# Mixture-of-experts up-projections as three float32r products of split operands, and the ternary weights in three in-place passes

## The reference

```
x = layernorm(x).reshape(1024, 512)
probs = softmax(x @ gate_w.T)              # 8 experts
topk_w, topk_idx = top_k(probs, 2)         # weights then normed to sum 1
h = silu(x @ w1[e]) * (x @ w3[e])          # w1, w3: (8, 512, 1024) float32
y = h @ w2[e]                              # w2: (8, 1024, 512) float32
out = sum over the two experts of topk_w * y
```

```
s = 1 / clip(mean(abs(w)), 1e-5)
w_q = clip(round(w * s), -1, 1) / s        # w_gate, w_up: (2048, 512); w_down: (512, 2048)
```

## Time and profile before

| | us |
|---|---|
| median of 3 runs | 1607.39 |
| runs | 1606.76, 1607.39, 1616.51 |
| span of the profiled execution | 1614.2 |
| mean granted clock of TensorE over it | 0.912 |

### The profile page before, as it was taken

How to read it: one execution, slowest core, us unless ns; L and a number is a source line. 1 busy time by engine, 2 the same in 40 slices (tenths; PEclk the granted TensorE clock), 3 DMA queues, 4 the chain that set the end, 5 groups by cost and what they waited for, 6 DMA issues and landing times.

```text
span 1614.2 us, 23219 instructions
## 1 busy us (share of the span) xinstructions
PE 1381.5 (86%) x8228; PEld 705.0 (44%) x8228; DVE 1002.9 (62%) x1708; ACT 820.5 (51%) x1176; POOL 425.7 (26%) x317
## 2 busy tenths in 40 slices
PE   8993888898847999999999999776777787779786
PEld 4441555555524444444444444333444343444333
DVE  6997999999974011110111101698989999885973
ACT  5775888888830111011110111218888898882574
POOL 1114100000004657999950000301111111110340
PEclk9996999999978999999999999887777777779998
DMA  9995354544247999999997996379887878883001
GB/s 290 295 292 142 89 133 113 134 113 117 63 157 277 385 350 370 370 396 399 404 365 295 317 354 261 110 157 201 167 174 152 171 155 179 156 149 79 1 1 52
DMA packets 452746, 338.40 MB, mean 210 GB/s; under 512 B 366360, under 2 KB 368408, under 8 KB 452032
## 3 DMA queue, kind: packets, MB, share of 16 engines
q1 hardware_dynamic: 438384, 291.31, 63.0%
q0 software_dynamic: 9920, 37.75, 6.3%
q10 hardware_dynamic: 4368, 8.39, 1.4%
HBM read 205.86 MB, written 38.01 MB: 151 GB/s over the span
## 4 chain that ended last, share of the span: by engine, by line
PE 52%; DVE 28%; issue 10%; ACT 5%; POOL 2%; DMA 2%; POOLq 0%; DVEq 0%; ACTq 0%
PE scores L1062 17%; DVE arena L1915 11%; PE bank L1080 9%; PE scores L1133 4%; PE bank L945 4%; DVE arena L1702 2%; PE scores L928 2%; PE scores L929 2%; PE bank L1180 2%; DVE arena L1688 2%; ACT arena L1377 2%; PE scores L1242 1%; PE bank L1278 1%; PE scores L1072 1%; PE scores L1162 1%
## 5 line engine op out<-in xcount | busy, mean ns | idle before, releaser
L1915 DVE TENSOR_SCALAR_CACHE_REDUCE arena<-scores,arena 128x1024 f32<-128x1024 f32 x256 | 314.6, 1279 | 32.0 <-PE scores L1133 30.6
L1062 PE MATMUL scores<-arena 128*128 128x512 f32 x736 | 319.7, 592 | 0.0
L1476 ACT ACTIVATE arena<-arena 128x2048 int16<-128x2048 f32 x128 | 273.6, 2149 | 78.5 <-POOL arena L828 41.9
L1838 DVE TENSOR_TENSOR arena<-scores,arena 128x512 f32<-128x512 f32 x46 | 31.8, 692 | 442.6 <-PE scores L1062 442.6
L1133 PE MATMUL scores<-arena 96*128 96x512 bf16 x512 | 193.2, 486 | 86.3 <-DVE arena L1915 81.6
L1062 PEld LDWEIGHTS scores<-arena 128*128 128x128 f32 x736 | 139.8, 190 | 175.8 <-issue 175.5
L1080 PE MATMUL bank<-arena 128*128 128x512 f32 x368 | 164.7, 601 | 3.4 <-issue 3.3
L1425 ACT ACTIVATE arena<-scores 128x512 f32<-128x512 f32 x46 | 27.5, 597 | 209.7 <-PE scores L1062 209.7
L1688 DVE TENSOR_REDUCE arena<-scores 128x1 f32<-128x640 f32 (+3 forms) x128 | 127.7, 1019 | 4.8 <-PE scores L906 4.4
L1377 ACT ACTIVATE arena<-scores 128x512 f32<-128x512 f32 (+3 forms) x256 | 116.6, 506 | 26.0 <-PE scores L929 25.0
L1702 DVE TENSOR_TENSOR arena<-arena 128x1024 f16<-128x1024 f32 (+2 forms) x128 | 126.2, 1026 | 3.5 <-ACT arena L1384 3.4
(11 more groups left out here) (285 smaller groups left out, 2160.0 us busy)
## 6 DMA issues: line engine op xcount, KB each, us to landing
arena<-in_L_ffn_w SPq DMA_DIRECT2D x69, 2048.0 KB, 12.6
arena<-arena SPq DMA_DIRECT2D x32, 256.0 KB, 2.9
kst_d<-arena POOLq DMA_DIRECT2D x16, 384.0 KB, 5.5
tern_d<-arena POOLq DMA_DIRECT2D x12, 512.0 KB, 7.0
arena<-kst_d SPq DMA_DIRECT2D x16, 384.0 KB, 4.0
xs_d<-arena SPq DMA_DIRECT2D x23, 256.0 KB, 2.9
arena<-xs_d SPq DMA_DIRECT2D x22, 256.0 KB, 13.0
ys_d<-arena ACTq DMA_DIRECT2D x22, 256.0 KB, 7.0
```

Of the source, the lines that this page charges most:

```text
L1062: ins = pe.matmul(scores[:, m * 1024 + half * 512:m * 1024 + half * 512 + 512], xsT[a][:, c], wa[:, m, c, half * 512:half * 512 + 512], st ...
L1476: act.activation(dst, src, ACT.Exp, bias=ebias[n % SBUFS], scale=-1.0, accum_out=rsum[h % 2][:, t:t + 1]).then_inc(p_ready, 1)
L1915: dve.tensor_scalar(ssb[i][:, s:s + 1024], scores[:, s:s + 1024], nsq[:, h, t:t + 1], None, ALU.mult, ALU.min, accum_out=nmx[i][:, half:ha ...
```

## The change

- The products for w1 and w3 are split. An operand a becomes hi = a rounded to float32r (a 4-byte type) and lo = a - hi; the product is hi*hi + hi*lo + lo*hi, so 48 products of 128x128 by 128x512 in float32r take the place of 16 in float32. The w2 products stay float32.
- w1 and w3 come in 92 pieces of 1 MB ([128, 2, 1024]); `raw` has 6 buffers for them, `whi` and `wlo` 3 each. ACT rounds a piece (`round_piece`), DVE takes the rest (`rest_of_piece`), each over 128x2048 float32. The turned rows of a slot are split in the same way (`round_slot`, `rest_of_slot`, 128x512). w2 comes in halves of 1 MB into 3 buffers.
- PE's order has the first piece of the next slot around the transposes of h. The slots are written out, with no loop, and four registers hold the experts.
- DVE splits pieces 0 and 1 within the routing steps.
- The ternary chunks come ahead of v on POOL, and both use one buffer: the load of a chunk is issued after the last pass over the one before. A chunk has three passes of two-operation tensor_scalar, the first two in place. The v passes become two-operation too.
- The transposes of `tern_d` for w_gate and w_up move from slots 20 and 21 to a place in the second attention, ahead of the load of Wp. Wq is loaded after POOL's last chunk.
- The mean of the weights moves from ahead of the routing into the first attention, with two DVE instructions for three.

```diff
@@ sync @@
+            def load_piece(n, e):
+                if n >= RAWS:
+                    sp.wait_ge(lo_done, n - RAWS + 1)
+                w = (w1, w3)[n % 2]
+                sp.dma_start(raw[:, n % RAWS], piece(w[bass.ds(e, 1)].rearrange("e (k p) n -> p (e k) n", p=P), n)).then_inc(raw_in[n % RAWS], 16)
+            def load_down(m, e):
+                if m >= DOWNS:
+                    sp.wait_ge(down_done, m - DOWNS + 1)
...
-                    if isinstance(u, int) and u in (SLOTS - 3, SLOTS - 2):
-                        w = u - (SLOTS - 3)
-                        for s in tern_stored:
-                            sp.wait_ge(s, 16 * 6)
-                        sp.dma_start_transpose(wT[w].rearrange("p o c n -> p (o c) n"), tern_d[w]).then_inc(wT_in, 16)
...
+            sp.wait_ge(v_made, 3 * NC // 4)
+            sp.wait_ge(tern_stored, 16 * TERN_CHUNKS)
             sp.dma_start(wq_sb, Wq.rearrange("(k p) n -> p k n", p=P)).then_inc(wq_loaded, 16)
...
             load_queries(1)
+            for w in range(2):
+                sp.dma_start_transpose(wT[w].rearrange("p o c n -> p (o c) n"), tern_d[w]).then_inc(wT_in, 16)
             sp.dma_start(wp_sb, Wp.rearrange("(k p) n -> p k n", p=P)).then_inc(wp_loaded, 16)
@@ gpsimd @@
+                pool.tensor_scalar(chunk, chunk, wst[:, 3, w:w + 1], MAGIC, ALU.mult, ALU.add).then_inc(w_step, 1)
+                pool.wait_ge(w_step, 2 * g + 1)
+                pool.tensor_scalar(chunk, chunk, MAGIC + 1.0, MAGIC - 1.0, ALU.min, ALU.max).then_inc(w_step, 1)
+                pool.wait_ge(w_step, 2 * g + 2)
+                if g:
+                    pool.wait_ge(tern_stored, 16 * g)
+                pool.tensor_scalar(tern, chunk, -MAGIC, 1.0, ALU.add, ALU.mult).then_inc(tern_made, 1)
+                pool.wait_ge(tern_made, g + 1)
+                pool.dma_start(tern_d[w][:, c * TERN_COLS:(c + 1) * TERN_COLS], tern).then_inc(tern_stored, 16)
...
-                f(pool.tensor_scalar(above, wchunk[a], wst[:, 3, w:w + 1], None, ALU.is_gt))
-                f(pool.tensor_scalar(below, wchunk[a], wst[:, 4, w:w + 1], None, ALU.is_lt))
-                pool.wait_ge(w_step, 2 * g + 2)
-                pool.tensor_tensor(tern[a], above, below, ALU.subtract).then_inc(tern_made, 1)
-                pool.tensor_scalar(vchunk[a], vchunk[a], MAGIC, None, ALU.add).then_inc(v_made, 1)
+                pool.tensor_scalar(vchunk, vchunk, MAGIC, 1.0, ALU.add, ALU.mult).then_inc(v_made, 1)
@@ tensor @@
+                for j in range(2):
+                    c = 2 * (i // 2) + j
+                    for x, w in ((xhi, whi), (xhi, wlo), (xlo, whi)):
+                        ins = pe.matmul(scores[:, s:s + 512], x[:, u % 2, c], w[:, n % SPLITS, j, cols],
+                                        start=c == 0 and x is xhi and w is whi, stop=c == KC - 1 and x is xlo)
...
+            up(0)
+            for u in range(SLOTS):
+                more = u + 1 < SLOTS
+                up(4 * u + 1)
+                if more:
+                    turn_slot(u + 1)
+                up(4 * u + 2)
+                up(4 * u + 3)
+                if more:
+                    up_half(4 * u + 4, 0)
+                turn_h(u)
+                if more:
+                    up_half(4 * u + 4, 1)
+                down(u)
@@ scalar @@
+                if n >= SPLITS:
+                    act.wait_ge(up_done, 2 * (n - SPLITS) + 2)
+                act.activation(whi[:, n % SPLITS], raw[:, n % RAWS], ACT.Copy).then_inc(hi_done, 1)
+            def slot(u):
+                more = u + 1 < SLOTS
+                if more:
+                    round_piece(4 * u + 4)
+                    round_slot(u + 1)
...
+                if more:
+                    round_piece(4 * u + 5)
...
+                if more:
+                    round_piece(4 * u + 6)
+                    round_piece(4 * u + 7)
...
@@ vector @@
+            def rest_of_piece(n):
+                dve.wait_ge(hi_done, n + 1)
+                dve.tensor_tensor(wlo[:, n % SPLITS], raw[:, n % RAWS], whi[:, n % SPLITS].bitcast(F32), ALU.subtract).then_inc(lo_done, 1)
+            def slot(u):
+                more = u + 1 < SLOTS
+                if more:
+                    rest_of_piece(4 * u + 4)
+                    rest_of_slot(u + 1)
...
+                if more:
+                    rest_of_piece(4 * u + 5)
...
+                if more:
+                    rest_of_piece(4 * u + 6)
+                    rest_of_piece(4 * u + 7)
```

More of the change, by code:

```diff
@@ L26 @@
 F32 = mybir.dt.float32
+F32R = mybir.dt.float32r
 BF16 = mybir.dt.bfloat16
@@ L307, in program @@
-        WCOLS = 4 * D
-        wchunk = [rw.take(F32, WCOLS) for _ in range(2)]
-        above, below = (rw.take(BF16, WCOLS) for _ in range(2))
-        tern = [rw.take(BF16, WCOLS) for _ in range(2)]
-        vchunk = [wchunk[a].rearrange("p (t d) -> p t d", d=D) for a in range(2)]
-        gath = Region(wbuf1_at, m_mark)
+        assert rm.at <= oatt_at + 4 * GT * D
+        over_xn = Region(m_mark, WT_AT)
+        wchunk_late = over_xn.take(F32, TERN_COLS)
+        tern_late = over_xn.take(BF16, TERN_COLS)
@@ new lines, in program @@
+        rs = Region(WT_AT)
+        xsin = [rs.take(F32, D) for _ in range(2)]
+        xhi = placed(F32R, "xhi", rs.at, 2, KC, P)
+        rs.at += 2 * 4 * D
+        xlo = placed(F32R, "xlo", rs.at, 2, KC, P)
+        rs.at += 2 * 4 * D
+        sg = rs.take(F32, EH)
+        hT = rs.take(F32, EC, P)
+        yb = [rs.take(F32, D) for _ in range(2)]
+        posi = rs.take(I32, 2, NT)
+        slot_e = rs.take(I32, SLOTS + 1)
+        r1 = [rs.take(F32, NT) for _ in range(10)]
+        vinv = rs.take(F32, D)
@@ L347, in program @@
         early = Region(WT_AT - 4 * D * (KC + 1), WT_AT)
-        assert early.at >= m_mark
+        assert early.at >= m_mark and rs.start >= early.end
         wq_sb = early.take(F32, KC, D)
@@ L812, in _ @@
+                pool.wait_ge(v_made, 3 * g + 3)
             assert SLOTS % 2
@@ L1075, in slot @@
                 for half, ready in enumerate((hT0_ready, hT1_ready)):
-                    pe.wait_ge(ready, at(u))
-                    if half == 0 and not first:
-                        pe.wait_ge(y_ready, at(u - 1))
-                    for c in range(4 * half, 4 * half + 4):
-                        ins = pe.matmul(bank7[:, :], hT[:, c], wb[:, c], start=c == 0, stop=c == EC - 1)
-                ins.then_inc(y_done, 1)
-            sweep(pe, SLOTS, slot)
+                    m = 2 * u + half
@@ L1439, in _ @@
                 act.activation(ohT[:, g * 512:(g + 1) * 512], bank[:, :], ACT.Copy).then_inc(ohT_ready, 1)
-            sweep(act, SLOTS, slot)
+            round_slot(0)
+            round_piece(2)
+            round_piece(3)
+            for u in range(SLOTS):
+                slot(u)
             def root(n, dst, src):
@@ L1729, in att_unit @@
                     split_m(u + 1, False)
+                if not past(u, 4) and u == 3:
+                    weight_means()
                 if last:
@@ L1849, in _ @@
             dve.reciprocal(vinv, svrow).then_inc(v_step, 1)
-            sweep(dve, SLOTS, slot)
+            for u in range(SLOTS):
+                slot(u)
             for t in range(NT):
```

365 lines of the change are left out of this document (212 added, 153 removed).

## The result

| | before | after |
|---|---|---|
| median, us | 1607.2 (4 runs) | 1582.45 (4 runs) |
| lowest to highest | 1606.76 to 1616.51 | 1580.14 to 1584.59 |
| span of the profiled execution | 1614.2 | 1580.7 |
| first gather starts at | 1004.32 | 964.06 |

A forecast was written before the change was run, and what follows sets the result against it. PE sets the experts' pace with DMA close behind, DMA binding while chunks run; 44 us gained and 16 lost give 28 off a 1614.2 span, 1586, and a 1579 us median (1554 to 1590, chance 0.57).

The forecast's parts named there:

- the gather: End of the expert slots: slot 21's y at 957, the gather at 960.5 instead of 1004.3, 44 us gained.
- The product: w1 and w3 products on PE: 0.216 us each, 48 in 10.35 us for 13.73, a slot of 19.1 us.
- ratio of four: Argument for the product's price: a float32 product costs four bf16 passes of 512 columns, so float32r takes one, 0.216 us.
- Rival 2: PE's products: no cheaper than a float32 record, 0.429 us each, a slot of 29.3 us, time 1770; chance 0.06.
- DMA: Expert slots: 410 GB/s ceiling, the bound at 20.3 us a slot while ternary chunks run, until 772 us.
- Splits and lock: ACT 1.95 and DVE 2.29 us a piece; DVE's subtractions waiting on POOL's passes cost 0.2 us a slot, 3 in all.
- Rival 3: Expert slots: short covers fail through the DVE-POOL lock or product joints, 1 us or more a slot, 1590 to 1605; chance 0.17.
- POOL's pass: Ternary pass on POOL: 2.5 us, bounded by 1.89 (the cast) and 5.45 (comparisons); POOL ends at 862 us.
- Rival 1: POOL holds the gather: passes of 5.4 us, POOL ending at 990 to 1030, time 1609 to 1650; chance 0.20.
- The start: Routing and first slots: piece 0 delays slot 1's rows to 520.4; slot 0's y at 538.4 instead of 529.3.
- The store of slot 21's y: End of the slots: 3.6 us of copy and store from y to gather; Wq lands long before its use.
- The transposes: Two 2 MB transposing loads before the first softmax tile: 2 x 7.9 = 16 us lost, ends 0 and 35.

The follow-up runs named there:

- their own experiment: The kernel before, with only the two transposing loads moved to their later place in the second attention: 16.8 us slower, 1624.37 us.
- bf16 experiment: The changed kernel with the high and low parts as bf16 instead of float32r: 1573.88 us, 8.6 us under the changed kernel.
- kernel with long passes: The changed kernel with the second operation of each of the three ternary passes left out (one-operation passes): 1585.85 us, gather at 965.20.
- The experiment: The changed kernel with DVE's subtractions of pieces 1 to 3 put behind the end of the scatter: 1584.35 us, gather at 964.2.
- paced kernels: The changed kernel with each ternary or v chunk on POOL waiting for 10 more product groups, spreading sixteen chunks over 20 slots: 1579.04 us.

## Why the prediction was right, point by point

The median is 1582.45, forecast 1579; 24.8 us gained for 28. Of the two terms, the gather moved by 40.3 us (forecast 44), and the transposes cost 16.8 us by their own experiment (forecast 16): 23.5. Both bounds of the slot, PE and DMA, and the price of the transposes came near the forecast. That the gather came within 3.6 us of the forecast is in part luck: errors of 3 to 5 us in several terms went opposite ways, as the points below show.

**The product.** Forecast 0.216 us, "one bf16 pass". It is 0.233, and the bf16 experiment shows that the type makes the difference. The 48 products take 11.16 us instead of 10.35, but the transposes and joints take 1.31 (0.44 and 0.87 in the chain) where I kept 1.85, so PE's slot is 19.34 instead of 19.1, 5 us over 21 slots instead of 17. My argument by the ratio of four gave the price of a bf16 pass and nothing in the rows tied float32r to it. Rival 2 was far off: three products cost 0.70 us, a float32 one 0.86.

**DMA.** Forecast: the bound while chunks run, 410 GB/s, 20.3 us a slot. Measured 416 to 418 GB/s and 20.08 us. The bound began about 640 us, not 538: until then PE was busy for 116 of 116 us. That pieces loaded ahead lasted that long is my reading; no run tried it. And it ended about 860 us, not 772: it held through v's chunks too, which I had not counted. So eleven slots were bound by DMA where I took 11.5, but not the same ones. The 21 slots took 414.7 us (541.55 to 956.3, the end of slot 21's w2), while my terms add to 417.9 (418.6 by the rounded 957): 5 more for PE's slot, 5 less for DMA (11 x 0.77 = 8.5 for 11.5 x 1.2 = 13.8), 3 less for the lock, which no step outside the DMA-bound ones shows.

**Splits and lock.** ACT 1.91 us for 1.95. DVE's median is 2.29 as forecast, with a tail to 6.6. (The DVE instruction of the earlier trace rows that I called a subtraction is a multiplication of two SBUF operands; the reading holds for it.)

```profile
L1531 ACT ACTIVATE whi<-raw 128x2048 fp32r<-128x2048 f32 x87 | 163.7, 1908 | 46.4 <-PE scores L1137 46.4
...
L1920 DVE TENSOR_TENSOR wlo<-raw,whi 128x2048 fp32r<-128x2048 f32 x87 | 208.4, 2416 | 153.3 <-ACT whi L1531 153.3
```

PE waited 1.4 us in all for these parts from 540 to 955 us, and the gather moved by 2.0 us where the ternary passes were left out; I had charged 3 for the lock. The lock fell on POOL instead: the first pass, 1.90 by its work, took 4.23 in the mean, and in none of the twelve less than 3.19, so it met a subtraction each time. The Trainium skill (SBUF — State Buffer, Who interferes with whom) calls this port an exclusive lock; the trace agrees, 5.39 us beside 1.90. Rival 3 did not come in the changed kernel. In the kernel with long passes, where PE waited 10.2 us, it came at 3.9 us in all, far from its 1 us a slot.

**POOL's pass.** My weakest term, 2.5 us between 1.89 and 5.45, is 1.90. Rival 1's price, 1609 to 1650, was too high. With ternary passes of 5.4 us POOL ended at 965, 25 us ahead of the 990 I summed, and held the gather by 0.6 us. By an estimate from these rows, v's passes at 5.4 us too would put back 8 x 2.1 = 17 us, so that the rival would have cost some 18 us, not 26 and more, and would have begun at a pass of about 5.0 us (18 us over 44 passes under 5.4), not 4.5.

**The start.** Slot 0's y is at 541.55, forecast 538.4. What I left out is that the subtractions hold up the scatter's issues: its sixteen take 22.9 us instead of 16.2, and PE turns slot 1's rows at 523.0 for the 520.4 of my sum. The experiment found nothing to gain there: without the hold-up the rows' load came into a queue, and the gather stayed.

**The store of slot 21's y.** I took 3.6 us from y to gather, as before. It is 7.8 (956.3 to 964.06), of which the landing is 6.2: SP and DMA rows of the changed kernel say why (KB, median us from issue to landing):

```profile
953.33 0.45 SPq L685 DMA_DIRECT2D arena<-in_L_xattn_Wq  x1
...
964.06 1.10 POOL L892 DMA_INDIRECT arena<-ys_d,arena  x1 [118.12 <-issue]
```

```profile
arena<-in_L_xattn_Wq SPq DMA_DIRECT2D x1, 1024.0 KB, 8.0
arena<-in_L_xattn_bq SPq DMA_DIRECT2D x1, 256.0 KB, 9.8
ys_d<-arena ACTq DMA_DIRECT2D x1, 256.0 KB, 6.2
```

Wq and bq, 1.25 MB, are issued from 3.7 us ahead of that store, which is issued at 956.99 and lands after 6.2 us where before it took 2.0. In the bf16 and paced kernels it takes 6.3 and 6.6. My step "Wq's load is now behind POOL's work on SP, and lands long before its use" looked at its user alone. The kernel with one-operation passes tests this without having been meant to: Wq is issued at 964.94 there, behind the store of 960.90, while the last load of w2 is 4.1 us ahead of the store as in the changed kernel, and the store lands after 2.8 us. So Wq and bq ahead of it cost 3.4 us, and 0.8 of the 4.2 lie elsewhere, perhaps in that load of w2. A kernel with Wq alone moved was not run. Together: 3.1 later at the start, 3.9 less in the slots, 4.2 more from y to gather, 3.6 us (by rounding) of the 44.

**The transposes.** Forecast 2 x 7.9 = 16 us. SP's row of the changed kernel has 16.44, with the first tile's transpose 22 us earlier than in the earlier trace rows for a gather 40 us earlier:

```profile
1052.76 16.44 SPq L721 DMA_TRANSPOSE arena<-tern_d  x2
...
1070.42 10.00 SPq L730 DMA_TRANSPOSE arena<-arena  x3
```

## What to carry to other kernels

A transfer moved out from under a long stage, where nobody waits, to the front of a chain must be priced by the time its issue holds its queue; cut into pieces and put where the queue idles, it was free. Where two resources are close (here PE 19.3 and DMA up to 20.1 us a slot), a delay of 1 to 2 us at the start of the stage did not show at its end, and spreading the transfers evenly brought the slots back to PE's pace. A load that nobody waits for yet is still to be priced by whom it delays: 3.4 us for the store behind it. For a price that no row has, name both nearest rows and ask which one each argument ties it to: POOL's pass came out at the row with its traffic (the cast) and not at the one with its instruction, and the float32r product at neither of its bounds.

## What the runs showed of the hardware

- POOL's tensor_scalar over 128x2048 float32: 1.90 us with two operations, 5.36 to 5.56 with one, in the same place of the same kernel. A second operation that does nothing is thus worth writing: v's addition took 5.37 us alone before, and 1.90 with a multiplication by 1 behind it after, where no subtraction held it up.
- A product of 512 columns takes 0.233 us in float32r, 0.216 in bf16 and 0.86 in float32, all at the full granted clock.
- A DVE subtraction of two SBUF operands holds up POOL's indirect DMA issue: 3.98 us beside it, 1.76 for the same one without it.
- A store of 256 KB lands after 2.8 us, and after 6.2 with 1.25 MB of loads issued 3.7 us ahead of it.
- A 2 MB transposing load holds SP for 8.2 us with little beside it, a 256 KB one for 1.4.
